# First phase of a convolution, linear-attention and FFN kernel: q and k parts turned by DMA instead of TensorE, scores of a tile in one stage, a PSUM bank of its own for the turned z, new stage orders on all five engines

## The reference

```
x = tpl_inv @ x                          # 128 x 128 over the channels, from a filter; then t = x as (16, 1024, 128)
n = (t - mean) / sqrt(var + eps)         # over the 128 channels
Q, K = elu(n @ W_q.T) + 1, elu(n @ W_k.T) + 1 ;  V = n @ W_v.T       # 8 heads of 16
S = cumsum_t(K_t V_t^T) ; z = cumsum_t(K_t)                          # causal linear attention
out = (Q S) / max(Q . z, 1e-6) ;  t = t + out @ W_out.T
x2 = (t - mean) / sqrt(var + eps)
g = mean_t(relu(x2 @ gfc1.T + b) @ gfc2.T + b2)                      # gate of a batch, 8 experts
W1, b1, W2, b2 += sum_e g_e * tv_..._e                               # FFN weights merged per batch
res = x2 + relu(x2 @ W1.T + b1) @ W2.T + b2
t = t + LN(res) * lng + lnb              # and back to (16, 128, 32, 32)
```

## Time and profile before

| | us |
|---|---|
| median of 3 runs | 897.52 (897.34 to 898.06) |
| profiled execution | 895.99 |
| its span, first to last instruction | 893.5 |
| PE / DVE / ACT / POOL busy | 821.2 / 775.7 / 744.2 / 593.1 |
| granted PE clock, mean | 0.986 |
| DMA: packets, bytes | 30305, 40.54 MB |

### The profile page before, as it was taken

One profiled execution on the slowest core, in us unless ns is written; L12 is line 12 of the kernel. 1 busy time (PEld: TensorE's weight loads), 2 busy tenths in 40 slices (PEclk: granted clock), 3 DMA queues, 4 the chain that ended last, 5 costly groups with the idle time before them and its releaser, 6 DMA issues. The chain is left out here.

```text
span 893.5 us, 39197 instructions
## 1 busy us (share of the span) xinstructions
PE 821.2 (92%) x12192; PEld 622.0 (70%) x12192; DVE 775.7 (87%) x2864; ACT 744.2 (83%) x1875; POOL 593.1 (66%) x1137
## 2 busy tenths in 40 slices
PE   1599999999999999999999999996899998799994
PEld 1277777777777777777777777775777777577773
DVE  6589999999999999999999999994688896588894
ACT  1489999999999999999999999983578885678884
POOL 5478898898888988988989889873023332033333
PEclk9999999999999999999999999997999999999998
DMA  2301010110110101101101111001012221112222
GB/s 75 84 9 55 26 41 23 53 35 29 35 53 23 41 29 47 41 23 41 47 29 35 32 45 41 23 19 36 1 38 72 86 78 59 49 37 84 82 70 82
DMA packets 30305, 40.54 MB, mean 45 GB/s; under 512 B 4044, under 2 KB 17519, under 8 KB 30200
## 3 DMA queue, kind: packets, MB, share of 16 engines
q1 hardware_dynamic: 30264, 40.01, 13.9%
HBM read 22.69 MB, written 17.30 MB: 45 GB/s over the span
## 5 line engine op out<-in xcount | busy, mean ns | idle before, releaser
L791 DVE SCALAR_TENSOR_TENSOR scores_lo<-p_a,scores_hi 128x512 f16<-128x512 f32 x256 | 163.8, 681 | 0.3 <-ACT scores_hi L691 0.2
L691 ACT ACTIVATE scores_hi<-p_a 128x512 f16<-128x512 f32 x256 | 148.1, 615 | 5.1 <-PE p_a L536 1.5
L871 POOL TENSOR_TENSOR qk_parts<-qk_f,qk_parts 128x128 f16<-128x128 f32 x256 | 111.1, 454 | 33.9 <-DVE qk_parts L772 33.9
L681 ACT ACTIVATE qkT_parts<-p_tr 128x1024 f16<-128x1024 f16 x128 | 131.4, 1027 | 0.7 <-PE p_tr L521 0.7
L1314 POOL TENSOR_TENSOR ffn_rstd_shift<-ffn_rstd_shift,consts 128x4 f32<-128x4 f32 x32 | 36.7, 1146 | 133.2 <-DVE ffn_rstd_shift L1273 133.2
L536 PEld LDWEIGHTS p_a<-qkT_parts 64*128 64x128 f16 x1024 | 57.5, 95 | 68.2 <-issue 68.2
L536 PE MATMUL p_a<-qkT_parts 64*128 64x128 f16 x1024 | 101.9, 220 | 0.0
L533 PE MATMUL p_a<-mask_bf,ident_bf 128*128 128x512 bf16 x256 | 99.4, 388 | 1.1
L1097 PE MATMUL psb<-merged_W_of_batch,h_hi 128*128 128x128 f16 x512 | 94.2, 220 | 4.1 <-DVE h_lo L1251 3.1
L1143 ACT ACTIVATE h_f<-psb,merged_b_of_batch 128x512 f32<-128x512 f32 x128 | 87.2, 713 | 11.4 <-PE psb L1078 11.2
L1251 DVE TENSOR_TENSOR h_lo<-h_f,h_hi 128x512 f16<-128x512 f32 x128 | 95.4, 785 | 1.2 <-ACT h_hi L1154 1.2
(11 more groups left out here) (198 smaller groups left out, 3246.9 us busy)
## 6 DMA issues: line engine op xcount, KB each, us to landing
x_f<-in_x SPq DMA_DIRECT2D x32, 256.0 KB, 2.8
t_rows<-t SPq DMA_DIRECT2D x64, 128.0 KB, 1.7
t_back<-t_rows SPq DMA_DIRECT2D x32, 256.0 KB, 2.7
out<-out_tile SPq DMA_DIRECT2D x32, 256.0 KB, 2.0
tv_share<-in_L_ffn_tv_W SPq DMA_DIRECT2D x32, 128.0 KB, 2.5
base_ffn_weights<-in_L_ffn_W SPq DMA_DIRECT2D x2, 256.0 KB, 4.2
W_hi_lo_rows<-base_parts SPq DMA_DIRECT2D x4, 128.0 KB, 3.9
consts<-in_consts SPq DMA_DIRECT2D x1, 300.5 KB, 2.8
```

Source lines behind the costliest of these rows:

```text
L681: nc.scalar.activation(qkT[:, t % 4, :, :, :].rearrange("p w a c -> p (w a c)"), p_tr[:, :, :, :].rearrange("p w a c -> p (w a c)"), ACT.C ...
L691: nc.scalar.activation(ah[:, t % 2, cols], p_a[:, cols], ACT.Relu).then_inc(ahi_ready[eo], 1)
L791: nc.vector.scalar_tensor_tensor(al[:, t % 2, cols], p_a[:, cols], 0.0, ah[:, t % 2, cols], ALU.max, ALU.subtract).then_inc(alo_ready[eo], 1)
L871: last = nc.gpsimd.tensor_tensor(lo, src, pk[:, t % 4, w, :, 0:DH], ALU.subtract)
```

## The change

- The stages `turn` (PE) and `copy_qk` (ACT) and the PSUM tile `p_tr` go. SP issues one `dma_start_transpose` per tile, `pk` (128 x 1024 float16) to `qkT`, with four semaphores, one for each buffer. It waits for `lo_ready`; the products of the scores wait for it.
- `scores_0` and `scores_1` become `scores`: both masks, then the eight products, alternating between rows 0 to 63 with bank 0 and rows 64 to 127 with bank 1.
- `qk_hi` (DVE) is split: `q_hi` on ACT, `k_hi` on POOL.
- `centre` and `normalise` (POOL) become one `normalise` on DVE, which subtracts and multiplies.
- `turn_z` writes to `p_m3`, a bank of its own. `read_t1` waits for a z that is one tile older.
- All stage orders are new. SP follows one too (`SYNC_ORDER`); the stores of the split base weights move behind batch 0.

```diff
-TENSOR_ORDER = [("scores_0", 3), ("scores_1", 3), ("turn", 2), ("turn_out", 5), ("conv", 0), ("values", 4),
-                ("gate", 8), ("turn_z", 7), ("project", 0), ("state", 1), ("out_project", 5)]
-SCALAR_ORDER = [("split_x", 0), ("z_hi", 8), ("exp_qk", 1), ("relu_qk", 1), ("read_t1", 6), ("tv_hi", 0),
-                ("v_hi", 1), ("scores_hi_0", 3), ("scores_hi_1", 3), ("copy_out", 5), ("copy_qk", 2),
-                ("gate_relu", 8)]
-VECTOR_ORDER = [("denominator", 5), ("read_state", 2), ("invert", 5), ("z_lo", 8), ("divide", 5),
-                ("make_qk", 1), ("stats2", 6), ("qk_hi", 1), ("stats1", 0), ("mean_var2", 6), ("tv_lo", 0),
-                ("v_lo", 1), ("mean_var1", 0), ("eps1", 0), ("eps2", 6), ("scores_lo_0", 3),
-                ("scores_lo_1", 3)]
-GPSIMD_ORDER = [("rsqrt2", 7), ("split_x", 0), ("state_hi", 2), ("normalise", 7), ("state_lo", 2),
-                ("qk_lo", 1), ("rsqrt1", 0), ("centre", 6)]
+TENSOR_ORDER = [("scores", 3), ("conv", 0), ("values", 4), ("gate", 8), ("turn_out", 5), ("turn_z", 7),
+                ("project", 0), ("state", 1), ("out_project", 5)]
+SCALAR_ORDER = [("split_x", 0), ("relu_qk", 1), ("exp_qk", 1), ("read_t1", 6), ("z_hi", 8), ("tv_hi", 0),
+                ("v_hi", 1), ("q_hi", 1), ("scores_hi_0", 3), ("scores_hi_1", 3), ("gate_relu", 8), ("copy_out", 5)]
+VECTOR_ORDER = [("normalise", 7), ("invert", 5), ("make_qk", 1), ("divide", 5), ("stats2", 6), ("read_state", 2),
+                ("stats1", 0), ("z_lo", 8), ("mean_var1", 0), ("mean_var2", 6), ("v_lo", 1), ("tv_lo", 0),
+                ("eps1", 0), ("eps2", 6), ("scores_lo_0", 3), ("scores_lo_1", 3), ("denominator", 4)]
+GPSIMD_ORDER = [("rsqrt2", 7), ("split_x", 0), ("state_hi", 3), ("k_hi", 1), ("state_lo", 3), ("qk_lo", 1),
+                ("rsqrt1", 0)]
+SYNC_ORDER = [("load_x", 3), ("load_tv", 3), ("store", 7), ("turn", 2)]
...
-                    def load(b, hf):
-                        q = 2 * b + hf
-                        at_least(sp, xh_ready, 2 * (q - 1))
-                        at_least(sp, xl_ready, 2 * (q - 1))
-                        sp.dma_start(xf[:, hf, :], d["x"][bass.ds(b * P, P), hf * HALF * P:(hf + 1) * HALF * P])\
+                    def load_x(b, t):
+                        if t % HALF:
+                            return
+                        hf = t // HALF
+                        sp.wait_ge(ones_set, 1)
+                        sp.wait_ge(xl_ready, TILES // 2 * b + 2 * (hf + 1))
+                        sp.dma_start(xf[:, hf, :], d["x"][bass.ds((b + 1) * P, P), hf * HALF * P:(hf + 1) * HALF * P])\
                             .then_inc(x_loaded[hf], 16)
 
-                    def load_tv(b):
-                        if not isinstance(b, int):
-                            sp.wait_ge(tv_split, b)
+                    def turn(b, t):
+                        n = TILES * b + t
+                        parts = n + 1 if isinstance(n, int) else sp.to_reg(n + 1)
+                        sp.wait_ge(ones_set, 1)
+                        sp.wait_ge(lo_ready, parts)
+                        sp.dma_start_transpose(qkT[:, t % 4, :, :, :].rearrange("p w a c -> p (w a) c"),
+                                               pk[:, t % 4, :, :, :].rearrange("p w h c -> p (w h c)"))\
+                            .then_inc(qk_turned[t % 4], 16)
+
+                    def load_tv(b, t):
+                        if t != 1:
+                            return
+                        sp.wait_ge(ones_set, 1)
+                        sp.wait_ge(tv_split, b + 1)
+                        tv_rows(b + 1)
+
+                    def tv_rows(b):
                         for i, src in enumerate((d["L1_ffn_tv_W1"].rearrange("e (i o) d -> (e i) (o d)", i=FI),
                                                  d["L1_ffn_tv_W2"].rearrange("e (i o) f -> (e i) (o f)", i=FI))):
                             sp.dma_start(tvs[:, i, :], src[:, bass.ds(b * TVW, TVW)]).then_inc(tv_loaded, 16)
 
-                    def store(b, pair):
+                    def store(b, t):
+                        if t % 2 == 0:
+                            return
+                        pair = t // 2
                         hf, i = pair // 2, pair % 2
+                        sp.wait_ge(ones_set, 1)
                         sp.wait_ge(t1_ready, TILES * b + 2 * (pair + 1))
                         sp.dma_start(d["t1"][bass.ds((2 * b + hf) * P, P), 2 * C * i:2 * C * (i + 1)],
                                      yt[:, 2 * pair:2 * pair + 2, :].rearrange("p a c -> p (a c)"))\
                             .then_inc(t1_stored[pair], 16)
 
-                    load_tv(0)
-
-                    for part, (done, src) in enumerate(((s_bhi, bwh), (s_blo, bwl))):
-                        sp.wait_ge(done, 1)
-                        sp.dma_start(d["base_parts"][part].rearrange("i p w -> p i w"), src[:, :, :])\
-                            .then_inc(base_stored, 16)
+                    tv_rows(0)
...
+                    stages = [(skew, {"load_x": load_x, "load_tv": load_tv, "store": store, "turn": turn}[name])
+                              for name, skew in SYNC_ORDER]
+                    no_loads = [(skew, {"store": store, "turn": turn}[name])
+                                for name, skew in SYNC_ORDER if not name.startswith("load")]
+                    batch(stages, 0, old=False)
+                    for part, (done, src) in enumerate(((s_bhi, bwh), (s_blo, bwl))):
+                        sp.wait_ge(done, 1)
+                        sp.dma_start(d["base_parts"][part].rearrange("i p w -> p i w"), src[:, :, :])\
+                            .then_inc(base_stored, 16)
...
-                    with sp.Fori(1, B) as b:
-                        load(b, 0)
-                        load_tv(b)
-                        store(b - 1, 0)
-                        store(b - 1, 1)
-                        load(b, 1)
-                        store(b - 1, 2)
-                        store(b - 1, 3)
-                    for pair in range(TILES // 2):
-                        store(B - 1, pair)
+                    with sp.Fori(1, B - 1) as b:
+                        batch(stages, b)
...
-                             {"turn_out": (oT_ready,), "turn_z": (zhi_ready, zlo_ready)}]
+                             {"turn_out": (oT_ready,)}, {"turn_z": (zhi_ready, zlo_ready)}]
...
-                    def turn(b, t):
...
-
-                    def scores(eo):
-                        def stage_(b, t):
-                            n = TILES * b + t
-                            pe.wait_ge(qkT_ready, n + 1)
+                    def scores(b, t):
+                        n = TILES * b + t
+                        for eo in range(2):
                             at_least(pe, ahi_ready[eo], n)
                             at_least(pe, alo_ready[eo], n)
-                            bank, r = p_a[:, eo * 512:(eo + 1) * 512], 64 * eo
-                            mm(bank, identb[:, :], maskb[:, :].unsqueeze(1).broadcast_to([P, NP, P]),
+                            mm(p_a[:, eo * 512:(eo + 1) * 512], identb[:, :],
+                               maskb[:, :].unsqueeze(1).broadcast_to([P, NP, P]),
                                start=True, stop=False, skip_group_check=True)
-                            for a in range(NP):
-                                last = mm(bank[:, a * P:(a + 1) * P],
+                        pe.wait_ge(qk_turned[t % 4], 32 * b + 16 * (t // 4 + 1))
+                        for a in range(NP):
+                            for eo in range(2):
+                                r, c0 = 64 * eo, eo * 512 + a * P
+                                last = mm(p_a[:, c0:c0 + P],
                                           qkT[r:r + 64, t % 4, 1, a, :], qkT[r:r + 64, t % 4, 0, a, :],
                                           start=False, stop=True, skip_group_check=True)
-                            last.then_inc(sc_done[eo], 1)
...
-                        at_least(act, z_ready, n - 1)
+                        at_least(act, z_ready, n - 2)
...
-                    def copy_qk(b, t):
-                        n = TILES * b + t
-                        act.wait_ge(tr_done, n + 1)
+                    def q_hi(b, t):
+                        n = TILES * b + t
+                        act.wait_ge(qk_ready, n + 1)
                         at_least(act, av_done, n - 3)
-                        nc.scalar.activation(qkT[:, t % 4, :, :, :].rearrange("p w a c -> p (w a c)"),
-                                             p_tr[:, :, :, :].rearrange("p w a c -> p (w a c)"), ACT.Copy)\
-                            .then_inc(qkT_ready, 1)
+                        src = qk[:, t % 4, 0:C].rearrange("p (h i) -> p h i", i=DH)
+                        dst = pk[:, t % 4, 0, :, :].rearrange("p h (a b i) -> p h a b i", a=2, b=2)[:, :, :, 0, :]
+                        nc.scalar.activation(dst, src.unsqueeze(2).broadcast_to([P, NH, 2, DH]), ACT.Copy)\
```

(52 more changed lines are left out.)

43 lines of the change are left out of this document (12 added, 31 removed).

## The result

The changed kernel takes 862.54 us (862.38 to 862.66, 4 runs) against 897.72 (897.34 to 898.06) on the same chip: ratio 0.9608, 95% interval 0.9591 to 0.9625. That is 35 us less, where 75 were forecast. The profiled span is 860.6 us at a mean granted clock of 0.979.

The account below looks back on a forecast made before the run. TensorE, 98.35% busy in a ring of waits with three other engines, was taken as the bound. Slot 4.44 to 3.85 saves 0.59 x 130 = 77 us; 893.5 - 77 + 2 = 818.5, as run median 823; range 795 to 940.

Parts of the forecast that it names:

- 3.76 down to 3.55: TensorE's us per slot: 4.44 less 0.46 for the turns and 0.22 for scores, lower if neighbouring products overlap.
- step (c): TensorE's scores: eight products alternating row halves and banks may run side by side, gaining between 0 and 0.21 us.
- 3.77: VectorE's us per slot: 4.44 less 0.87 for qk_hi plus 0.2 for normalise.
- 0.2 with a ceiling of 0.25: Cost in us of the new normalise on VectorE, sized from the two-operand z_lo; floor 0.1.
- 3.67: ScalarE's us per slot: 4.44 less 1.12 for copy_qk plus 0.35 for q_hi.
- 3.68: GpSimd's us per slot: 3.91 busy, less centre and normalise (0.91), plus 0.08 overlap and 0.6 for k_hi.
- under 3.3: Turning DMA's hold on SP's queue in us per transfer; below this it is hidden.
- under 5.0: Turning DMA's landing: 5.0 us from lo_ready to first product; each us beyond adds about 0.45 to a slot.
- B: Rival: SP makes the turned blocks one by one and becomes the bound, slot 4.0 to 4.3, 842 to 880 us; chance 0.15.
- C: Rival: turning transfers don't overlap, each holding the queue until landed; slot up to 5.0 us, 970 us; chance 0.20.
- The sum: Slot length: dearest engines 3.76 and 3.77, plus 0.08 for four engines holding each other up, taken as 3.85 us.
- D: Rival: p_in's readers before the next projection close an equally long ring; slot near 4.4, 890 to 900 us; chance 0.06.

Follow-up runs that it names:

- e1: Changed kernel with normalise moved from VectorE to ScalarE, and a 128 x 1 shift with two SBUF inputs added on VectorE: 868.12 us.
- e5: Changed kernel with normalise on ScalarE and its 128 x 1 shift on VectorE made from one SBUF tensor and a scalar: 867.67 us.
- e4: Changed kernel with a second turning DMA per tile, into a buffer that nobody reads: 866.61 us.
- e12: Kernel before the change with the scores in one stage and nothing else changed: 871.64 us.
- e16: Changed kernel, normalise on ScalarE, VectorE's order with invert, divide, shift ahead of make_qk, and z_lo, mean_var2 ahead of stats1: 841.87 us.

## Why the prediction was half right

- **TensorE**, 3.76 down to 3.55. The turns are gone. The scores stage takes 304.71 - 303.86 = 0.85 us, the lower bound of step (c): neighbours do run beside each other, eight in the 0.33 us that four took (row halves and banks alternate together, so no run tells which of the two it needs). Both stages came out as forecast. Busy is 0.919 x 4.17 = 3.83 by the windows, above my 3.76; the windows count the tail of the last product before a wait as busy (ahead of `values` at 305.37 they show 0.32 us idle, though the product before it had started at 304.83), so they can't decide between 3.55 and 3.76. That PE has 8% of slack is plain.
- **VectorE**, 3.77. `qk_hi` went, but **`normalise` was mis-sized**: mean 534 ns, some 0.46 in pitch, where I took 0.2 with a ceiling of 0.25. The rows say why: at 303.79 it runs 0.70 us and ends 0.08 behind the `x_lo` on GpSimd that ended at 304.41; at 307.74 it takes 0.42 and ends 0.08 behind `state_hi` (307.61 + 0.47). Where it starts 0.13 us ahead of the GpSimd instruction, as at 328.68, it takes 0.34, and that `x_lo` 0.74 instead of 0.67. The Trainium skill, SBUF — State Buffer, SBUF: two separate sides, says that VectorE in a two-port mode or with two SBUF inputs and GpSimd take a shared pair of ports as an exclusive lock, whoever starts first. The trace agrees, to 0.05 us of start (at 312.01 `normalise` is recorded 0.05 ahead of `x_lo` and still takes 0.80, ending 0.08 behind it), and e1 and e5 show it on one instruction: 0.62 us with two SBUF inputs beside `x_lo`, 0.21 as one source and a scalar. I had not weighed that rule; the change moves an instruction of this kind against a GpSimd 81% busy. Yet it is not where the 40 us went: e5 took 0.22 us a slot off DVE and gained nothing.
- **ScalarE**, 3.67: `q_hi` is 419 ns, busy 0.857 x 4.17 = 3.57. **GpSimd**, 3.68: `k_hi` 397 ns, at the floor, not the 0.6 taken; busy 0.811 x 4.17 = 3.38. Both are right or better.
- **DMA.** Hold on the queue 1.25 us (under 3.3), landing 3.1 (under 5.0, inside 2.8 to 4.2). The share of the DMA engines went from 0.11 to 0.46, not to the 0.3 or so that 102 GB/s instead of 38 alone would give (0.11 x 102 / 38): 165,473 packets against 30,305. It had room (e4: 0.80 at no slot cost). Rivals B and C fell. That the measured time lies inside B's 842 to 880, and inside my range up to 940, is luck: SP's queue is held 1.25 us a turn, and not by eight blocks one by one. The Trainium skill, VectorE: DVE Perf Modes, The three transpose paths, has 1309 ns for one 128 x 128 block; here eight blocks in one instruction were there after 3.1 us, so they don't go in series. For what its page Advanced Engine Details and Errata, X-Bar Transpose (TRN2), says, that turning runs at the speed of other DMAs: 3.1 us against 2.7 for 256 KB plain, nearly.
- **The sum: this step failed.** "Four engines so near each other hold each other up now and then ... I add 0.08." The dearest engine stands at 3.97 and the slot at 4.17; with DVE at 3.75 and ACT at 3.87 (e5) the slot was 4.21. So the term is 0.20 to 0.34 above the busiest engine, not 0.08. Of the 0.32 us a slot that were missing (4.17 for 3.85), 0.20 stand under DVE (3.97 for 3.77) and 0.12 here; but with the 0.20 taken away again (e5) the slot stayed, so it was this term that decided. I had looked at one ring (D: the readers of `p_in` before the next projection) by its wait in the earlier trace rows and gave it 0.06. What came is of that kind but through other stages: two closed chains over four engines, each as long as the slot in all 48 slots of the window (3.97 us in the one shown, 4.17 in the mean). In the kernel before, PE at 98% set the slot; whether such chains lay just behind it, no run shows. The lists were in the diff and most durations in the trace before, so both chains could have been added up ahead, roughly.
- **What the parts were worth.** The scores stage alone some 25 us (e12), then DVE is full at 98%; the rest of the change takes some 0.3 to 0.4 us from DVE, 0.7 from ACT and 0.5 from POOL, and gives 10 more. Of what remained to my forecast, some 20 us were in the order of DVE's list together with `normalise` on ACT (e16). Still open are 19 us between e16 (841.9) and 823: PE is 95% busy there, DVE 95, ACT 95, with waits of 3 to 7 us in 200 for one another; whether a better order or only less work removes them, no run shows.

## What to carry to other kernels

When one full engine is relieved, the new length of a slot need not be that of the next busiest engine: write down each closed chain (a buffer or a position in a list that leads back to the next tile), add the durations along it with the hand-overs, and take the longest; expect it to tell where to look, not how much comes of it. A chain binds where every start along it follows the end before it by the same short hand-over, slot after slot (here 0.1 us), even if the profile lists no wait. Where two are equally long, an edit that opens one shows nothing; try them together before the theory is dropped. An order should be laid for the chain that goes through `make_qk`-like points where several engines wait for one instruction: what can be later (`normalise`) goes behind it or behind what feeds others (`divide`).

## What the runs showed of the hardware

- Eight 64-row products alternating between the row halves and between two banks take 0.33 us in all, as long as four in one half.
- A DMA that turns eight 128 x 128 float16 blocks SBUF to SBUF: 1.25 us on the queue, 3.1 us to land; two per tile land in 3.3 and 3.1 us at a DMA share of 0.80.
- A 128 x 1 instruction on VectorE with two SBUF inputs takes 0.15 to 0.64 us (median 0.35, e1), 0.20 to 0.22 as one input and a scalar (e5).
